# Filling every slot of TensorE's program up to 768 instructions with waits that are already met

## The reference

```python
for l in range(6):
    qkv = x @ Wqkv[l]                       # 128 -> 3 * 1024
    q, k = l2norm(q) * qs, l2norm(k) * ksc  # per head of 64
    q = q * cos * scale + rotate_half(q) * sin * scale
    k = k * cos * inv + rotate_half(k) * sin * inv
    out = softmax(8.0 * q @ k2.T, masked to the window and the one before) @ v2
    x = x + out @ Wo[l]
    h, gate = split(norm(x) @ W1[l] + b1[l])
    x = x + (h * gelu(gate)) @ W2[l] + b2[l]
```

## Time and profile before

| | |
|---|---|
| three timed runs | 2112.93, 2114.34, 2118.89 us; median 2114.34 |
| the profiled execution | 2119.18 us, of which the span from first to last instruction is 2117.4 us |
| busy, share of the span | PE 92%, PEld 68%, DVE 86%, ACT 73%, POOL 61% |
| granted TensorE clock, mean | 0.984 |
| PE matmuls, weight loads | 37572 of each |
| instruction queues | q8: 299 packets, 4.90 MB; q14: 100 packets, 0.82 MB |

### The profile page before, as it was taken

The page is one execution under the profiler, slowest core; times in us unless marked ns, Lnnn a source line. Parts: engine busy times, 40 slices in busy tenths (PEclk is TensorE's granted clock), DMA queues, the critical chain, the costliest instruction groups (busy, mean ns, idle before and its releaser), DMA issues.

```text
span 2117.4 us, 89360 instructions
## 1 busy us (share of the span) xinstructions
PE 1943.4 (92%) x37572; PEld 1442.3 (68%) x37572; DVE 1821.4 (86%) x3995; ACT 1546.8 (73%) x3028; POOL 1290.5 (61%) x1551
## 2 busy tenths in 40 slices
PE   6888899987788999999999999999999999999996
PEld 4666664455566777777777777777777777777774
DVE  6788775577798999999899999999999998998994
ACT  4777763355576877888788887888878878777873
POOL 1111110000378888788787888878888887777771
PEclk9999999998899999999999999999999999999998
DMA  5000000100232322332333323333233332222321
GB/s 117 2 2 2 2 32 31 61 1 1 58 86 70 79 68 70 93 84 67 78 83 78 87 65 77 86 89 79 67 81 83 87 75 63 73 75 73 77 63 41
DMA packets 99377, 132.62 MB, mean 63 GB/s; under 512 B 29052, under 2 KB 44034, under 8 KB 98978
## 3 DMA queue, kind: packets, MB, share of 16 engines
q1 hardware_dynamic: 98978, 126.90, 23.6%
HBM read 28.20 MB, written 1.11 MB: 14 GB/s over the span
## 4 chain that ended last, share of the span: by engine, by line
PE 48%; DVE 23%; ACT 10%; issue 9%; SPq 5%; POOL 3%; DMA 2%; DVEq 0%; POOLq 0%; ACTq 0%
PE pj L630 15%; PE oo L630 15%; ACT arena L1961 7%; PE sc L630 6%; PE tr L1057 5%; DVE arena L1764 4%; DVE arena L1766 4%; SPq L555 3%; PE tr L633 3%; DMA slab<-arena 2%; DVE bv L1772 2%; DVE arena L1521 2%; DVE small L1795 1%; DVE xn L1353 1%; ACT L1965 1%
## 5 line engine op out<-in xcount | busy, mean ns | idle before, releaser
L1961 ACT ACTIVATE arena<-tr 128x512 f32<-128x512 f32 (+3 forms) x894 | 458.8, 562 | 100.0 <-PE tr L633 51.3
L2397 POOL TENSOR_TENSOR arena<-arena 128x1024 f32<-128x1024 f32 x192 | 457.4, 2382 | 91.3 <-DVE arena L1766 87.5
L1961 ACT ACTIVATE arena<-pj 128x512 f32<-128x512 f32 x576 | 332.5, 599 | 150.9 <-PE pj L630 96.1
L2415 POOL TENSOR_TENSOR arena<-arena,small 128x1024 f32<-128x1024 f32 x192 | 365.6, 1904 | 28.1 <-POOL small L2408 0.9
L1961 ACT ACTIVATE arena<-arena 128x1024 f32<-128x1024 f32 (+4 forms) x446 | 304.6, 693 | 87.6 <-DVE arena L1521 74.0
L1772 DVE TENSOR_REDUCE bv<-arena 128x8 f32<-128x512 f32 x384 | 252.7, 679 | 2.9
L630 PE MATMUL oo<-slab,arena 64*32 64x64 f32 (+1 forms) x12416 | 232.7, 229 | 10.5 <-issue 9.7
L2364 POOL TENSOR_SCALAR rstd<-mv 128x4 f32<-128x4 f32 x40 | 11.4, 284 | 364.5 <-DVE mv L1347 364.4
L633 PE MATMUL tr<-ident,arena 128*128 128x128 f32 x1346 | 206.4, 280 | 19.4 <-DMA beta<-in_L_attn_betas 9.9
L630 PEld LDWEIGHTS oo<-slab,arena 64*32 64x32 f32 (+1 forms) x12416 | 160.8, 106 | 80.0 <-issue 44.4
L633 PEld LDWEIGHTS tr<-ident,arena 128*128 128x128 f32 x1346 | 163.3, 143 | 58.3 <-issue 23.9
(11 more groups left out here) (340 smaller groups left out, 4465.0 us busy)
## 6 DMA issues: line engine op xcount, KB each, us to landing
slab<-arena SPq DMA_DIRECT2D x576, 128.0 KB
slab<-arena SPq DMA_DIRECT2D x336, 64.0 KB
arena<-gate_mem SPq DMA_DIRECT2D x24, 256.0 KB, 4.4
wqkv<-in_L_ffn_Wqkv SPq DMA_DIRECT2D x36, 128.0 KB, 2.5
arena<-in_L_ffn_Wqkv SPq DMA_DIRECT2D x36, 128.0 KB, 2.3
wo<-in_L_ffn_Wo SPq DMA_DIRECT2D x24, 128.0 KB, 2.5
w<-in_L_ffn_W SPq DMA_DIRECT2D x6, 341.0 KB, 3.6
YT<-in_L_attn_x SPq DMA_DIRECT2D x4, 256.0 KB, 3.9
```

The lines of the kernel that those rows point to most:

```text
L1961: return nc.scalar.activation(o, i, f, **k)
L2397: p_.tensor_tensor(r_, r_, rb[:, k, :], ALU.add).then_inc(sum_ok, 1)
L2415: p_.tensor_tensor(r3, r3, rs[:, k, :].unsqueeze(2).broadcast_to([P, HL, DL]), ALU.mult).then_inc(qk_rdy, 1)
```

## The change

In the tile stage TensorE gets extra waits on `ld_const` and `ld_late`, in three groups: behind `queries(0)`, behind `wo_quarter` and behind `queries(1)`. Their number is chosen slot by slot so that, with them, each slot from the third on has 768 instructions on TensorE (two or three instructions more or less at the borders between blocks). Each turn of the loop writes two conditions, and these become one EVENT_SEMAPHORE. The table gives 53, 55, 55 and 34 of them for t = 0 to 3, and 0, 0, 70, 66, 66, 67, 67 and 48 in the first eight slots: 384 + 22 x 197 = 4718 in all. A group is a third, rounded down; the third group has the rest: 17, 17 and 19 for t = 0, 18, 18 and 19 for t = 1 and 2, 11, 11 and 12 for t = 3.

```diff
+SPARE_AT = (53, 55, 55, 34)
+SPARE = {0: 0, 1: 0, 2: 70, 3: 66, 4: 66, 5: 67, 6: 67, 7: 48}
...
+            def spread_out(n):
+
+                for _ in range(n):
+                    pe.wait_ge(ld_const, n_const)
+                    pe.wait_ge(ld_late, n_late)
+
             def slot(s_):
...
+                spare = SPARE.get(g, SPARE_AT[t])
...
                 queries(0)
+                spread_out(spare // 3)
                 if s_.mw is not None:
...
                     wo_quarter(s_.mw, s_.iw)
+                spread_out(spare // 3)
                 if t == 3 and m1 is not None:
...
                 queries(1)
+                spread_out(spare - spare // 3 * 2)
                 if g > 0:
                     crossing(g, 1)
```

## The result

The changed kernel takes 2239.04 us (median of four runs, 2237.36 to 2242.45) against 2116.61 us of the kernel before on the same chip: ratio 1.0578, 95% interval 1.0548 to 1.0608, 122 us slower. The profiled execution took 2242.45 us with a span of 2240.6 us.

A forecast was written before the change was run, and what follows sets the result against it. TensorE and VectorE were both taken as close to full, with TensorE's sequencer decisive. Lateness 163 us, less 20 slack and 27 fetch, gave +116 and 2230 us; forecast range 2190 to 2265 (58%), 80% range 2160 to 2285.

The forecast's parts named there:

- The price of a wait: TensorE's sequencer: each added, already met wait takes 0.11 us from start to start; 4718 take 519 us, partly hidden.
- the rival that made the kernel faster: Waits close up to 0.051 us each and the fetch was the larger loss: 2086 us, chance 6%.
- The lateness of the steps: Output projection, turn of probabilities and down-projection start late where groups outlast the sequencer's lead: 6.7 us per four slots, 147 us.
- The first eight slots: Start of the tile stage: their 384 waits, in groups of 22 to 24, lose 16 us.
- What is given back: Tile stage: 20 us of TensorE's waits for other engines and 27 us of late instruction fetches are won back.
- The slack: TensorE's 91 us of waits for other engines in the tile stage: 20 us absorbed, bounds 0 and 91.
- The fetch: Long TensorE idles taken as late instruction packets, 35 us: fixed borders at 768 a slot win 27, bounds 0 and 35.
- the second border: Packet border in the second half of the values; its packet was to have some 4 to 5 us of a slot.
- VectorE as the bound: VectorE is the real bound, so TensorE's slack absorbs all 91 us and all 35 are won: 2151 us, chance 12%.
- Nothing is given back: Fetches stay late at the same borders in every slot and no wait shrinks: +163, 2277 us, chance 12%.
- The fetch was hidden anyway: The long idles could be the sequencer's own pace, so no fetch gain: +143, 2257 us, chance 12%.

The follow-up runs named there:

- the spread kernels: Against the changed kernel: same waits per slot over seven places, none between second queries and turn; versions with shifted fetch borders: 2163.52, 2116.42 and 2120.27 us.
- the first spread kernel: Changed kernel with its waits spread over seven places of each slot, 768 instructions kept: 2163.52 us, ratio 1.0237 to the kernel before.
- the second: As the first spread kernel, with 64 waits taken out of the third slot, so later fetch borders stand 64 instructions further along: 2116.42 us, ratio 0.9999.
- the fastest: As the second spread kernel, with the 34 waits of t = 3 slots all ahead of the wait for the probabilities: 2112.75 us, ratio 0.9976.

## Why the prediction was right

**The price of a wait** (0.11 us, bounds 0.099 and 0.121): 0.106 in unbroken runs. No run closed up to 0.051, and with that the rival that made the kernel faster falls.

**The lateness of the steps.** The first three columns of the table add up to 1.74 us more than before with t = 0, 2.61 with t = 1, 1.88 with t = 2 and 0.07 with t = 3. The prediction had 1.9, 2.4, 1.9 and 0.5: 6.7 us for four slots, measured 6.30, so 139 instead of 147 us. With t = 3 the down-projection starts 1.26 us behind the first transpose (1563.90 and 1565.16 us) instead of 1.02, 0.24 us late and not 0.5, and of that 0.08 us is left at the turn (3.04 and 2.96 in the table). With t = 1 the output projection is 0.95 us late and not 0.8. That each group costs at its own step is shown by the two kernels that have only some of them, and that the third costs most by the one in which it was moved: 104 us.

**The first eight slots.** The slots from 8 on account for (1.21 + 2.27 + 1.39 - 0.01) x 22 = 107 us, and 122 - 107 = 15 remain for all else, against 16. The ninth slot (number 8) starts at 718.17 us instead of 704.09, so 14 of the 15 lie in the first eight indeed.

**What is given back** was 47 us in the prediction and is 32 (139 - 107), and here the two parts were wrong in themselves, in opposite directions. Behind the turn a slot takes 0.06 us less up to the values, 0.24 us more from the values to the scores, and 0.55 less from there to the next slot: times 88 that is -5, +21 and -48 us.

- The slack (20 us, bounds 0 and 91). The other engines' waits in the weight loads fell from 91 to 19 us, but 25.5 of that is the renaming told above. What went for certain is the idleness that ScalarE ended in the scores (14.8 to 5.7) and in the turns of L1060 (12.9 to 1.7), and such pieces. By what is left when the fetch is counted (below), it was near the middle of its bounds and not 20. The kernel now leaves VectorE and ScalarE waiting longer. Waits of the two, kernel after; before, the first was 44.6 and the second 41.5 us:

```profile
ACT arena L1974 <- PE tr L636: 132.1, 93, 4.5
...
DVE arena L1777 <- ACT arena L1974: 109.4, 125, 1.7
```

- The fetch (27 us, bounds 0 and 35) is the step that failed. The prediction held that the second border, in the values, and the third have 4 to 5 us each, and that their stalls would go. The stall of the scores did; a new one of 0.5 to 1.0 us came into the second half of the values in most slots, as in the row at 1522.01. It is a packet that comes late. The view of DMA has no instruction packet from 1517.05 to 1519.75, and in the 0.05 us behind it this one:

```profile
q8 instruction: 1, 0.02, 122.6%
```

1.226 x 16 x 0.05 us are 0.98 us: it lands at 1520.75, and the values go on 1.3 us later. The border before it stands in the turn of probabilities, dispatched by 1517.0. So the sequencer passed into a packet at 1517.0, ran through its 256 instructions by 1521.3 with the long wait L1108 in between, and the next was there at 1522.0. 4 to 5 us were not enough.

The same can be counted over the whole stage. In the kernel before, one idle time of the earlier trace rows stands at 1510.83 us, and the view of DMA from 1508.30 to 1508.35 has:

```profile
q8 instruction: 1, 0.02, 146.9%
```

This packet took 1.17 us and landed at 1509.5, again 1.3 us ahead. Of the 34 idle times of weight loads over 0.65 us that are put down to issue (640 to 2050 us), 32 end 1.2 to 1.6 us behind the landing of a packet of TensorE's queue, 32.4 us together; a moment taken at random stands so in 9% of cases. So the prediction read the earlier trace rows rightly, and its 35 us were close. In the kernel after (640 to 2170 us) there are 56 such, 47.1 us, 53 of them in the values. The fetch gave nothing back and took about 15 us more, and what is left of the return, 32 + 15 = 47 us, came from elsewhere: an estimate, as a stall can also cover another wait. In the spread kernels these stalls are 80 with 78 us in the first, 21 with 19 us in the second, and 6 with 6 us in the fastest.

From the first spread kernel to the second, by place alone, the ratio goes from 1.0237 (+50 us) to 0.9999, and it is 0.9976 (-5 us) where the waits of t = 3 were moved as well. The bounds should have reached above zero: that a border stays in one place can be bad as well as good.

The Trainium skill (Runtime: NRT & Kernel Launch, "Instruction fetch mechanics") calls crossing into a block "mostly hidden". The 18 packets more for 4718 waits agree with its 16 KB; in the kernel before, 32 stalls over 0.65 us for 253 packets agree with "mostly" too. 80 stalls for 272 packets in the first spread kernel, and the 47 us between it and the second, whose instructions differ by 64 waits, show that by the place of the borders much can stay unhidden.

The rivals: none of the four. *The kernel gets faster* needed waits that close up, and they didn't. VectorE as the bound would have given 2151; moving one group took 104 us away with VectorE's work unchanged, so it didn't bind the changed kernel. "Nothing is given back" (2277) is 38 us above. "The fetch was hidden anyway" comes nearest in time (2257), but its reason, that the idles are not the fetch, is wrong. The sum was right to 6 us (+116 against +122) partly by luck: the lateness came out 8 us smaller and the return 15 us smaller, and inside the return a fetch term of the wrong sign stood against a slack that was put at less than half. The price of a wait and where it falls due were right on their own.

## What to carry to other kernels

A wait that is already met only takes sequencer time. It cost next to nothing here as long as the sequencer was ahead of the array, and beyond that it made the next step late: read the lead at each place (the time at which the sequencer passes a wait against the start of the step behind it), and spread such waits by it. Of the places tried, the one at which the sequencer has 1.0 us of lead was the worst for 19 in a row; ahead of a wait at which it stands 1.4 us anyway the kernel was no slower for them. To bring a loop to whole fetch packets gained nothing by itself: it fixes where the borders stand, and the place has to be tried, as 32 instructions turned 5 us of gain into 13 of loss. To know whether long idle times are late packets, compare their ends with the landings of the instruction queue's packets.

## What the runs showed of the hardware

A met wait on TensorE's sequencer costs 0.106 us from start to start, twice its recorded 51 ns, in long runs as in pairs. An instruction packet of 16 KB took 0.9 to 1.8 us of transfer in the kernels before and after, and where TensorE stood for one, it went on 1.2 to 1.6 us after the landing (1520.75 and 1522.01, 1500.7 and 1501.98, 1509.5 and 1510.83). Where 256 instructions passed in 2.7 us, it stood for 1.0 us. Why a packet's transfer begins when it does (here 2.7 us behind the border) is open; a long wait of the sequencer just behind a border goes with a late one in this trace, but the kernels with other places of the borders changed more than that, and none isolates it.
